# A rebuilt prologue: loads in sets, a smaller shear, the fifth chunk among the row tiles, near offsets and late weights loaded piece by piece

## What is computed

```
xn = layernorm(x)
q, k, v = heads(xn @ Wq + bq), heads(xn @ Wk + bk), heads(xn @ Wv + bv)      # 16 heads of 16
q, k = rotary(q), rotary(k)
att = softmax(causal((q @ k.T + rel_bias[bucket(i - j)]) / 4))
a = (att @ v) @ Wp + bp
logits = l2norm(xn) @ l2norm(col_emb).T + sigmoid(gelu(xn @ gate_w1 + b1) @ gate_w2 + b2)
weights = onehot(argmax(logits)) * softmax(logits)                            # one of 16 columns
f = layernorm((gelu(xn @ W_cols + b_cols) * weights) @ proj_w + proj_b + xn) * ln_g + ln_b
out = x + a + f
```

## Time and profile before

| | before |
|---|---|
| median of 3 runs | 2019.31 us (2018.33 to 2022.06) |
| the profiled execution | 2020.97 us |
| its span, first to last instruction | 2019.2 us |
| TensorE matmul busy | 1838.5 us, 91% |
| VectorE busy | 1602.9 us, 79% |
| ScalarE busy | 1112.2 us, 55% |
| GpSimd busy | 647.7 us, 32% |
| mean granted TensorE clock | 0.975 of 2.4 GHz |
| DMA | 184.97 MB, mean 92 GB/s |

### The profile page before, as it was taken

The page is one execution under the profiler, slowest core; times in us unless marked ns, Lnnn a source line. Parts: engine busy times, 40 slices in busy tenths (PEclk is TensorE's granted clock), DMA queues, the critical chain, the costliest instruction groups (busy, mean ns, idle before and its releaser), DMA issues.

```text
span 2019.2 us, 34843 instructions
## 1 busy us (share of the span) xinstructions
PE 1838.5 (91%) x10854; PEld 1022.5 (51%) x10854; DVE 1602.9 (79%) x5475; ACT 1112.2 (55%) x2146; POOL 647.7 (32%) x848
## 2 busy tenths in 40 slices
PE   4778999999999999999999999999999999999977
PEld 1445555555555545555555555555445555545433
DVE  2467888888888888888888888888888888778783
ACT  2324555665555566655566655555665555655544
POOL 5742223333322333332233333223333323311110
PEclk9789999999999999999999999999999999999997
DMA  8741322332233322333223322333223332222101
GB/s 223 217 124 58 90 81 70 116 97 77 82 90 102 91 89 82 93 93 105 69 83 116 94 81 83 90 99 94 89 81 94 92 100 67 80 85 69 59 12 48
DMA packets 216963, 184.97 MB, mean 92 GB/s; under 512 B 61931, under 2 KB 196475, under 8 KB 216780
## 3 DMA queue, kind: packets, MB, share of 16 engines
q1 hardware_dynamic: 216780, 182.75, 30.5%
HBM read 115.23 MB, written 72.94 MB: 93 GB/s over the span
## 4 chain that ended last, share of the span: by engine, by line
PE 64%; DVE 21%; issue 5%; ACT 5%; DMA 2%; SPq 2%; POOL 1%; DVEq 0%; ACTq 0%; POOLq 0%
PE o_bank L1069 11%; PE rows L1085 11%; PE scores L1052 9%; PE bank L1155 9%; PE scores L1144 8%; PE bank L1098 7%; DVE maxima L1242 4%; DVE scores L1216 4%; PE bank L1173 3%; ACT probs L937 3%; DVE rows L1237 2%; PE scores L1146 2%; DVE left L1351 1%; PE scores L1106 1%; DMA x<-in_x_dram 1%
## 5 line engine op out<-in xcount | busy, mean ns | idle before, releaser
L937 ACT ACTIVATE probs<-scores 128x512 f32<-128x512 f32 (+1 forms) x1280 | 672.5, 555 | 552.2 <-DVE scores L1216 313.1
L1242 DVE TENSOR_REDUCE maxima<-rows 128x1 f32<-128x384 f32 (+4 forms) x896 | 479.6, 551 | 174.2 <-PE rows L1085 173.3
L1052 PE MATMUL scores<-stack_q,stack_k 99*128 99x512 bf16 (+3 forms) x1536 | 436.0, 333 | 76.2 <-ACT probs L937 69.1
L1085 PE MATMUL rows<-stack_k,stack_q 96*128 96x256 bf16 (+3 forms) x2048 | 462.2, 292 | 14.7 <-DVE maxima L1242 4.5
L1237 DVE CUSTOM_DVE_ANT_0 rows<-rows,near_rows 128x256 f32<-128x256 f32 (+1 forms) x1024 | 393.9, 431 | 45.3 <-PE rows L1085 42.5
L1085 PEld LDWEIGHTS rows<-stack_k,stack_q 96*128 96x128 bf16 x2048 | 176.4, 98 | 356.0 <-issue 129.8
L1216 DVE TENSOR_TENSOR scores<-scores,near_cols 128x256 f32<-128x256 f32 x768 | 323.9, 432 | 18.3 <-PE scores L1052 17.5
L1069 PE MATMUL o_bank<-probs,v_aug 128*32 128x512 f32 (+3 forms) x3072 | 318.9, 503 | 2.8 <-ACT probs L937 2.8
L1155 PE MATMUL bank<-w_proj,act_t 128*128 128x256 f32 x1024 | 256.2, 383 | 23.1 <-DVE y L1272 23.1
L1144 PE MATMUL scores<-again,w_cols 128*128 128x256 f32 x1024 | 274.0, 390 | 0.0
L1052 PEld LDWEIGHTS scores<-stack_q,stack_k 99*128 99x128 bf16 x1536 | 142.3, 98 | 233.1 <-ACT probs L937 161.6
(11 more groups left out here) (112 smaller groups left out, 2001.4 us busy)
## 6 DMA issues: line engine op xcount, KB each, us to landing
parts_d<-part SPq DMA_DIRECT2D x96, 256.0 KB, 2.3
stack_q<-parts_d SPq DMA_DIRECT2D x384, 64.0 KB, 2.9
stack_k<-parts_d SPq DMA_DIRECT2D x384, 64.0 KB, 2.7
kept_d<-kept SPq DMA_DIRECT2D x31, 512.0 KB, 2.9
again<-kept_d SPq DMA_DIRECT2D x31, 512.0 KB, 3.5
x<-in_x_dram SPq DMA_DIRECT2D x32, 256.0 KB, 3.4
v_d<-v SPq DMA_DIRECT2D x32, 256.0 KB, 2.4
rest<-in_x_dram SPq DMA_DIRECT2D x32, 256.0 KB, 4.3
```

The lines of the kernel that those rows point to most:

```text
L937: act.activation(probs[:, (g * NS + s) % PROBS, h, 0:width], ring[(rings + ring_n[1]) % RING][:, 0:width], ACT.Exp, scale=float(D) ** -0.5 ...
L1052: ins = pe.matmul(ring[(rings + ring_n[1]) % RING][:, c0:c0 + w], stack_k[g % 2][:, h, kb * P:(kb + 1) * P], stack_q[g % 2][:, h, q0:q0 + ...
L1085: ins = pe.matmul(tile[:, at:at + k1 - k0], stack_q[ag % 2][0:STACK, h, qb * P:(qb + 1) * P], stack_k[ag % 2][0:STACK, h, k0:k1], start=Tr ...
L1242: ins = dve.tensor_reduce(maxima[:, part, m:m + n], tile[:, at:at + n * w].rearrange("p (n w) -> p n w", w=w), AX.X, ALU.max)
```

## The change

It rewrites the prologue; `iteration` and the stages of the loops stay, but for tests on negative g.

- *Loads in sets.* The five loads that the offset table and the embedding norm need go out on ACT's queue (`setup_in`), x of chunk 0 first on SP's, then five loads for q and k (`qk_weights_in`), x of chunk 1, and the other eleven (`weights_in`). Each engine waits for a set only where it first reads it. ACT no longer waits for the offset table's trip to DRAM (the table is made in `y`, not in `rot`); the memsets of `v_aug` move from POOL to DVE; the sum of two biases on POOL moves to `skip` of chunk 0.
- *Late weights.* W_cols in two pieces behind chunks 0 and 1, then Wp, proj_w and b_cols behind chunk 2.
- *Smaller shear.* `sheared_d` holds 32 copies in place of 128, and each near load becomes four, of 32 partitions. The rows of the first group load during chunk 1; the other twelve loads follow the last quarter of the stack.
- *Rotary.* For chunks 0 to 3 POOL turns q only, and a new stage `turn` turns k on DVE, in four operations a tile.
- *Order.* The chunks 0 to 3 follow each other with no neurons or rows between. The second half of the stack is loaded in two quarters (`load_part`). Then come the neurons of chunk 0 with the 12 early row tiles; the front of chunk 4 with 12 `MIDDLE` tiles, which need 768 rows; the columns of chunk 0, the back of chunk 4 and half the neurons of chunk 1 with 16 `LAST` tiles; and the shift with the other half.

```diff
+MIDDLE, LAST = (3, 5, 6), (4, 7, 8, 9)
+FIRST_ROWS = [(h, k) for ks in (EARLY, MIDDLE, LAST) for h in range(GH) for k in ks]
+FIRST_MIDDLE, FIRST_LAST = (0, MIDDLE[0]), (0, LAST[0])
+SHEARED = 32
...
+FIRST = ["stats", "center", "x_turn", "qk_begun 0", "qk 0", "turn 0", "qk_begun 1", "qk 1", "turn 1", "v 0", "v 1",
+         "hidden", "gate"]
...
-    between(-5, {})
-    between(-4, {"middle 1": [("load_q", -2, None), ("load_k", -2, None)],
-                 "next hidden": [("skip", -2, None)]})
-    pieces = [[(stage, -2, arg) for stage, arg in NEURONS[k:k + N_PIECES]] for k in range(0, len(NEURONS), N_PIECES)]
-    between(-3, {**dict(zip(("next x_turn", "next qk 0", "next qk 1", "next v 1"), pieces)),
-                 "middle 1": [("load_q", -1, None), ("load_k", -1, None)], "next gate": [("rest_in", -1, None)]})
-    early = len(EARLY) * GH
-    rows = [[("row", -1, row) for row in ALL_ROWS[k:k + 2]] for k in range(0, early, 2)]
-    between(-2, {**dict(zip(("choose", "left 0", "middle 0", "next qk 1", "next v 1", "next gate"), rows)),
-                 "middle 1": [("load", -2, None), ("load_v", -2, None)]})
-    plan = [(stage, int(arg[0]) if arg else None) for stage, *arg in map(str.split, FINAL) if stage not in FRONT_BEHIND]
-    plan += [("y2_stats", None), ("ffn_in", None), ("load", None), ("widen", None), ("finish", None)]
-    plan += [("skip", None), ("load_v", None), ("stats", None)] + NEURONS + [("center", None)]
-    for stage, arg in [("columns", k) for k in range(C_PIECES)]:
-        o.add(stage, -1, arg)
-    done = early
-    for at, (stage, arg) in enumerate(plan):
-        o.add(stage, 0 if stage in FRONT_AHEAD else -1, arg)
-        upto = early + (len(ALL_ROWS) - early) * (at + 1) // len(plan)
-        for row in ALL_ROWS[done:upto]:
-            o.add("row", -1, row)
-        done = upto
-    o.add("shift", -1)
-    o.add("shift_turn", -1)
...
+    between(-5, {"next gate": [("skip", -2, None)]})
+    between(-4, {"next v 1": [("load_q", -2, None), ("load_k", -2, None)]})
+    between(-3, {"next v 1": [("load_part", -2, 2)]})
+    early, last = GH * len(EARLY), GH * len(LAST)
+    rows = FIRST_ROWS[:early], FIRST_ROWS[early:-last], FIRST_ROWS[-last:]
+    neurons = [[(stage, g, arg) for stage, arg in NEURONS] for g in (-2, -1)]
+    columns = [("columns", -1, k) for k in range(C_PIECES)]
+    spread(each(-2, "qk_turn 0, left 0, middle 0, qk_turn 1, left 1, middle 1") + [("load_part", -2, 3)], [])
+    spread(neurons[0] + each(-1, "center"), rows[0])
+    spread(each(-2, "choose, load_v") + each(-1, "x_turn, qk_begun 0, qk 0") + each(-2, "tie")
+           + each(-1, "qk_begun 1, qk 1") + each(-2, "choice") + each(-1, "v 0, v 1, load_q, load_k, rest_in")
+           + each(-2, "mask_turn") + each(-1, "hidden, gate"), rows[1])
+    spread(columns + each(-1, "choose, qk_turn 0, left 0, middle 0, y2_stats, ffn_in, qk_turn 1, left 1, middle 1, tie, "
+                          "load, skip, widen, load_v") + [("stats", 0, None)] + neurons[1][:4], rows[2])
+    spread([("shift", -1, None)] + neurons[1][4:] + each(-1, "finish, shift_turn") + [("center", 0, None)], [])
...
-        sheared_d = nc.dram_tensor("sheared_d", (2, H, P, SHEAR), F32, kind="Internal").ap()
+        sheared_d = nc.dram_tensor("sheared_d", (2, H, SHEARED, SHEAR), F32, kind="Internal").ap()
...
+        def swaps(t, c, lanes):
+            n = (lanes.stop - lanes.start) // (GH * D)
+            q5 = qk[:, t, lanes].rearrange("p (g h s e) -> p g h s e", h=GH, s=2, e=D // 2)
+            r5 = rot[:, t, lanes].rearrange("p (g s e h) -> p g h s e", h=GH, s=2, e=D // 2)
+            return [(ALU.mult, (r5[:, :, :, s, :], q5[:, :, :, 1 - s, :], turned(c, t, 2 - s, n))) for s in range(2)]
+        def by_cos(t, c, lanes):
+            n = (lanes.stop - lanes.start) // D
+            q4 = qk[:, t, lanes].rearrange("p (h s e) -> p h s e", s=2, e=D // 2)
+            return q4, q4, rotary[:, c * CT + t, 0, :].rearrange("p (h s e) -> p h s e", h=1, s=1) \
+                .to_broadcast((P, n, 2, D // 2))
+        def added(t, lanes):
+            r4 = rot[:, t, lanes].rearrange("p (g d h) -> p g h d", h=GH, d=D)
+            return r4, qk[:, t, lanes].rearrange("p (g h d) -> p g h d", h=GH, d=D), r4
...
+            qk_weights = [
                 (w_qkv[:, :, 0:C], a["Wq"].rearrange("(k p) n -> p k n", p=P)),
                 (w_qkv[:, :, C:2 * C], a["Wk"].rearrange("(k p) n -> p k n", p=P)),
+                (b_qkv[:, 0:C], every(a["bq"], C)), (b_qkv[:, C:2 * C], every(a["bk"], C)),
+                (rotary[:, :, :, :], a["rotary"])]
+            first_weights = [
...
+            late_weights = [(w_cols[:, k, :].rearrange("p (c n) -> p c n", n=N),
+                             a["W_cols"][:, k * P:(k + 1) * P, :].rearrange("c p n -> p c n")) for k in range(KC)]
+            late_weights += [
+                (w_out[:, :, :], a["Wp"].rearrange("(k p) n -> p k n", p=P)),
+                (w_proj[:, :, :], a["proj_w"].rearrange("(m p) n -> p m n", p=P)),
+                (b_cols[:, :], bass.AP(a["b_cols"].tensor, 0, [[1, P], [P, EM]]))]
...
+            load_x(0, 0)
+            for dst, src in qk_weights:
+                sp.dma_start(dst, src).then_inc(qk_weights_in, 16)
+            load_x(0, 1)
             with nc.allow_non_contiguous_dma(reason="one bias per partition, once"):
-                for dst, src in first_in:
+                for dst, src in first_weights:
                     sp.dma_start(dst, src).then_inc(weights_in, 16)
-                load_x(0, 0)
-                load_x(0, 1)
-                sp.dma_start(w_out[:, :, :], a["Wp"].rearrange("(k p) n -> p k n", p=P)).then_inc(columns_in, 16)
-                sp.dma_start(w_proj[:, :, :], a["proj_w"].rearrange("(m p) n -> p m n", p=P)) \
-                    .then_inc(columns_in, 16)
-                for k in range(KC):
-                    sp.dma_start(w_cols[:, k, :].rearrange("p (c n) -> p c n", n=N),
-                                 a["W_cols"][:, k * P:(k + 1) * P, :].rearrange("c p n -> p c n")) \
-                        .then_inc(columns_in, 16)
-                sp.dma_start(b_cols[:, :], bass.AP(a["b_cols"].tensor, 0, [[1, P], [P, EM]])) \
-                    .then_inc(columns_in, 16)
             sp.sem_inc(result_out[0], 16)
             sp.sem_inc(result_out[1], 16)
...
+            for r in (1, 0):
                 sp.dma_start(sheared_d[r], bass.AP(offsets_d.tensor, r * (H * N_OFF + P),
...
+                                                   [[N_OFF, H], [0, SHEARED], [1, SHEAR]])).then_inc(sheared, 16)
+            def load_late(first, last):
+                with nc.allow_non_contiguous_dma(reason="one bias per partition, once"):
+                    for dst, src in late_weights[first:last]:
+                        sp.dma_start(dst, src).then_inc(columns_in, 16)
+            def load_near(r, near, first, last, landed):
+                for p in range(0, P, SHEARED):
+                    sp.dma_start(near[p:p + SHEARED, first:last, :],
+                                 bass.AP(sheared_d.tensor, (r * H + first) * SHEARED * SHEAR + P - r - p,
+                                         [[SHEAR - 1, SHEARED], [SHEARED * SHEAR, last - first], [1, 2 * P]])) \
+                        .then_inc(landed, 16)
...
+                    elif stage == "load_part":
+                        landed = quarter_in if arg == 2 else stack_in[0]
+                        for i in range(3):
+                            sp.wait_ge(parts_out[i], (arg + 1) * 16)
+                        alone(sp)
+                        times = slice(arg * CH, (arg + 1) * CH)
+                        for of, at, stack in ((Q_PARTS, 0, stack_q), (K_PARTS, KC, stack_k)):
+                            for r in range(2 * 3):
+                                src = parts_d[0, of[r], at, 0:GH * D, times].rearrange("(d h) t -> d h t", d=D)
+                                sp.dma_start(stack[0][r * D:(r + 1) * D, :, times], src).then_inc(landed, 16)
+                        if arg == NC - 1:
+                            load_near(0, near_cols, 0, GH, near_in)
+                            load_near(1, near_rows, GH, H, near_in)
+                            load_near(0, near_cols, GH, H, near_in)
...
+                        if g == 1 - LEAD:
+                            sp.wait_ge(sheared, 32)
+                            load_near(1, near_rows, 0, GH, near_first)
...
-                        if g == 1 - LEAD:
-                            load_near()
+                        if g < -2:
+                            load_late(g + LEAD, g + LEAD + 1 if g < -3 else LATE_LOADS)
...
-            for i in range(2):
-                fills += [(v_aug[i][:, :, :, :], 0.0), (v_aug[i][:, :, :, D:D + 1], 1.0),
-                          (stack_k[i][STACK:STACK + 3], 1.0)]
...
-            pool.wait_ge(weights_in, LOADS * 16)
```

(52 more changed lines are left out.)

135 lines of the change are left out of this document (82 added, 53 removed).

## The result

The changed kernel takes 2005.12 us (median of 4 runs, 2003.4 to 2009.64) against 2019.76 (median of 4 runs) for the one before: a ratio of 0.9931 [0.9915, 0.9946], 14.6 us less. The forecast was 36.3 less, and 1985 with a range of 1971 to 2001; the result lies outside. The profiled execution took 2005.78 us, with a span of 2004.0.

The account below looks back on a forecast made before the run. The loops were taken as TensorE-bound and unchanged, the 170.3 us prologue as a chain of waits, ending last on SP. First score at 134 instead of 170.3 takes 36.3 us off 2020.97, giving 1985, range 1971 to 2001.

Parts of the forecast that it names:

- The wait for x: Prologue, chunk 2: the 23.49 us wait for the third x load disappears with the smaller shear and late weights.
- Rival 4: Prologue: near loads of 32 partitions crawl at 60 GB/s, first score at 175, slower than before; chance 0.03.
- Rivals 2 and 5: 2: SP not late, first score 121, 1972 us, chance 0.16. 5: first score moves, end does not, near 2016, 0.04.
- Rival 3: Prologue: TensorE stays at half clock, another 4 us in each of four chunks, first score 150, 2001 us; chance 0.10.
- The turn: Chunks 1 to 3, centring to next centring or gate: 14.5 us each, gate of chunk 3 at 72.5.
- the base: Chunk pipeline: an undisturbed turn, read from chunk 2 of the earlier trace, lasts 14.3 us.
- the tile: VectorE's four rotary operations on one tile in chunks 0 to 3: 1.4 us.
- the upper bound of 3.9: VectorE's rotary cost per tile if each of its four operations waits for a GpSimd one: 1.4 + 2.5 us.
- Rival 1: Chunks: rotary halves on VectorE and GpSimd exclude each other, 17.3 us a chunk, first score near 142, 1993 us; chance 0.17.
- SP's chain: SP's queue from chunk 3's v, near 70.7, to the rest load landing at 109.5 to 115.7; first score 130 to 136.5.
- The work behind the last `left`: End of prologue: last rows, tie and statistics 7.0 us (7.5 on TensorE), then 5.1 and 4.8 to the first score.
- The late weights at nothing: Prologue: SP issues the last near 70, neurons want them near 74; priced at nothing, 0 to 4 us of wait possible.

Follow-up runs that it names:

- The version with four edits and the large shear: Changed kernel with rest load and last three late weights earlier, rotary halves back on GpSimd, last four near loads later, shear for 128 partitions: ratio 0.9899.
- the second profile: The changed kernel run and profiled again, unaltered: ratio 0.992, first score at 160.7 us.

## Why the prediction was wrong

*What held.* The loops kept their length. SP's path did end last, and the rest load with GpSimd behind it was its end. The wait for x went. Rival 4 fell: near pieces of 32 partitions, 384 KB each, landed in 7.0 and 12.7 us, where 60 GB/s for the 3.6 MB would have taken 60. Rivals 2 and 5 fell. Rival 3 named the clock, in another place.

*The turn was mis-sized: 17.0 to 18.3 us, not 14.5, and the gate of chunk 3 11.6 us late* (2.1 of them before the first turn, 9.5 in three turns). Two terms of that step failed, the base and the tile. Without the halves three turns came to 48.5 us, where 3 x 14.3 = 42.9 was taken: 5.6 of the 9.5. The halves added 4.5 to three turns, where 3 x 0.2 = 0.6 was taken: the other 3.9.
- The base. I took the 14.3 us of the earlier trace rows for an undisturbed turn. With GpSimd turning everything, as there, turns in the new prologue took 16.7 and 16.5. The version with four edits and the large shear centres chunk 2 at 53.64 and chunk 3 at 67.78: 14.1 us again, behind a wait of 6.4 us for x. So 14.3 is a turn behind a wait. That GpSimd used the wait to catch up fits it, but was not measured by itself. With the halves on VectorE it does not hold: in the changed kernel with the large shear the turn behind a wait of 7.7 us for x took 18.1.
- The tile. By the earlier trace rows a tile was 1.4 us. It is 1.66 with GpSimd quiet, 1.98 in the mean with its rotary work away and 2.61 beside it. The 0.26 is for the most part the sum operation, which reads and writes every fourth element and takes 0.63 us at its shortest where the cosine operation of as many columns takes 0.43 and the earlier trace rows has 0.42: the row that I drew the line through had another access pattern. The other 0.95 is GpSimd. That price stood in the prediction only as the upper bound of 3.9.

Rival 1 has the right turn (17.3) and a part of the mechanism: 3.9 us a tile was too much, 2.61 was measured, and the rest of the turn came from the base. The first tile pair of the changed kernel (timelines of VectorE and GpSimd, first and last operation of each):

```profile
23.29 0.85 DVE L1390 TENSOR_TENSOR rot<-qk,rotary 128x128 f32<-128x128 f32 x2
...
24.67 1.03 DVE L1395 TENSOR_TENSOR rot<-qk,rot 128x256 f32<-128x256 f32 x1
```

```profile
23.33 1.03 POOL L901 TENSOR_TENSOR rot<-qk,rotary 128x128 f32<-128x128 f32 x2 [4.22 <-DVE qk L1380]
...
25.30 1.13 POOL L906 TENSOR_TENSOR rot<-qk,rot 128x256 f32<-128x256 f32 x1
```

GpSimd needed 3.1 us (23.33 to 26.43) and VectorE was done inside them. Had each waited for the other's whole instructions, VectorE's 1.66 us and at least 2.1 of GpSimd's (the prediction's bound, half of the earlier trace rows) would stand one after the other: 3.8 as an estimate. The Trainium skill (SBUF — State Buffer, "Who interferes with whom") says that such instructions exclude each other for their whole length. This trace does not bear that out beside GpSimd's rotary operations, which cost VectorE 0.63 us a tile. Beside the subtraction `part` it nearly does: the sums of 1.55 and 1.46 us both ended 0.48 behind it, where 0.63 would be a whole sum. GpSimd's spans are rough.

*SP's chain was mis-sized: 50.1 us from v to bias, not about 43* (134, less 17.6 behind the start of `left`, 2.6 on GpSimd and the 70.7 of v). The stack loads were right (7.5 for twelve), the parts between them took 2.8 instead of 1.5. The near issues took 8.3 us instead of 6.0, and the four issues behind them 9.4 instead of 2.0: 9.7 for the full queue, where the sum allowed 0 to 6.2 and about 4 of it went into the 134. The upper bound of the earlier trace rows was right in kind and too low.

*The work behind the last `left` took 20.6 us, not 17.6* (to the shift turn at 151.52 it was 16.3 instead of 12.8, behind it 4.4 instead of 4.8). TensorE came back from 7.42 us of idle time at half clock, and the first neuron stage took 2.46 us where 1.40 was the step: 1.1 us are shown to be the clock's, the rest was not separated. In the second profile it took 23.8, with three such stages. I had given the slow clock a price in the chunks only.

Together: 11.8 us at the start of SP's chain (82.5 instead of 70.7), 7 in it, 3 behind it, and that is the 21.9 us between 134 and 155.9. The late weights at nothing held for the kernel as changed (0.36 us). That they were the next bound, by 2.6 us, only showed when the halves were undone.

## What to carry to other kernels

Where one queue issues everything in a fixed order, write down who waits for each transfer and when, and move the single issue that ends last; put no megabytes ahead of any load that an engine is about to need. A consumer in its own program order must not be moved ahead with it. Before a gap between two events is taken as the length of a step, look whether a wait stood ahead of it. Price an operation from a row with the same access pattern and with the same neighbour at work; the neighbour was the larger part here. Take a tile's price from busy time, since means of operations that overlap count the overlap twice. Undo each part twice, once as it stands and once with the last bound out of the way: halves and shear each moved a stage by 5 us and the end by nothing, and only one of them was worth something afterwards.

## What the hardware showed that was not expected

An SP issue that takes 0.34 to 0.5 us with room in the queue (kept_d 0.50 at 73.69) took 4.88 behind 3.5 MB of near loads. A VectorE sum of 256 columns through strided views took 0.63 us with GpSimd quiet, 1.11 in the mean beside its rotary work and 1.55 beside one subtraction of 512 columns, where plain views took 0.42. And one kernel's two profiles differed by 4.8 us at the first score, 3.2 of it behind the last `left`: TensorE came back from 7.42 us of idle time in one and 8.08 in the other, and ran one full neuron stage at half clock in the first and three in the second.
